# Seeding PSUM bank by bank in a graph-network kernel, with a wait for each bank

## The reference

```python
mask = (adj > 0.0).astype(x.dtype)
xj_proj = x @ W1a
diff = x[:, :, None, :] - x[:, None, :, :]
h = jax.nn.relu(xj_proj[:, :, None, :] + diff @ W1b + b1)
hm = jnp.einsum('bjkh,bjk->bjh', h, mask)
deg = jnp.sum(mask, axis=-1)
return hm @ W2 + deg[..., None] * b2
```

## Time and profile before

| what | value |
|---|---|
| time, median of 3 runs | 905.02 us (904.84 to 905.02) |
| the profiled execution | 904.65 us, of which the span from first to last instruction is 902.6 us |
| busy share | TensorE 96%, VectorE 96%, ScalarE 86%, GpSimd 77% |
| seeds (L530) | 512, 811 ns each |
| granted TensorE clock | 0.983 of full speed |

### The profile page before, as it was taken

The page is one execution under the profiler, slowest core; times in us unless marked ns, Lnnn a source line. Parts: engine busy times, 40 slices in busy tenths (PEclk is TensorE's granted clock), DMA queues, the critical chain, the costliest instruction groups (busy, mean ns, idle before and its releaser), DMA issues.

```text
span 902.6 us, 27715 instructions
## 1 busy us (share of the span) xinstructions
PE 862.0 (96%) x8626; PEld 771.7 (86%) x8627; DVE 866.4 (96%) x3032; ACT 775.9 (86%) x1728; POOL 698.8 (77%) x1548
## 2 busy tenths in 40 slices
PE   3879999999999999999999999999999999999996
PEld 1448999989998989999999999998999899989995
DVE  6989999999999999999999999999999999999993
ACT  4858989898989898989889898988898889898983
POOL 0857787888888888888887878787878788888874
PEclk9789999999999999999999999999999999999997
DMA  9700000000000000000000000000000000000000
GB/s 341 279 1 5 20 11 20 16 20 17 19 17 20 11 20 17 20 17 20 15 14 16 20 17 19 17 18 18 12 20 16 20 16 20 16 20 11 7 8 16
DMA packets 26549, 27.58 MB, mean 31 GB/s; under 512 B 3360, under 2 KB 24352, under 8 KB 25376
## 3 DMA queue, kind: packets, MB, share of 16 engines
q1 hardware_dynamic: 25488, 25.37, 8.3%
q10 hardware_dynamic: 912, 0.39, 0.2%
HBM read 21.56 MB, written 4.19 MB: 29 GB/s over the span
## 4 chain that ended last, share of the span: by engine, by line
PE 69%; DVE 19%; issue 5%; ACT 3%; POOL 2%; DMA 1%; SPq 0%; ACTq 0%; POOLq 0%; DVEq 0%
PE ring L378 36%; DVE acc L763 12%; PE ring L406 6%; PE post L465 4%; PE post L464 4%; PE prep L435 4%; PE post L470 4%; PE prep L445 3%; PE prep L442 2%; DVE onehot_space L749 2%; PE prep L441 2%; ACT ring L530 1%; POOL rstd L915 1%; DMA x_all<-x_nbf_dram 1%; DVE onehot_row L804 1%
## 5 line engine op out<-in xcount | busy, mean ns | idle before, releaser
L763 DVE SCALAR_TENSOR_TENSOR acc<-ring,acc 128x384 f32<-128x384 f32 x896 | 489.0, 546 | 1.1 <-PE ring L378 0.2
L530 ACT COPY ring<-P 128x768 f32<-128x768 f32 x512 | 403.3, 811 | 16.3 <-DVE acc L763 6.9
L378 PE MATMUL ring<-PQ,onehot_space 128*128 128x192 f16 x4096 | 404.0, 247 | 7.2 <-ACT ring L530 3.3
L378 PEld LDWEIGHTS ring<-PQ,onehot_space 128*128 128x128 f16 x4096 | 338.2, 100 | 31.7 <-ACT ring L530 19.2
L864 POOL TENSOR_TENSOR relu_row<-relu_row 128x192 f32<-128x192 f32 x256 | 151.8, 593 | 101.1 <-ACT relu_row L562 91.1
L749 DVE TENSOR_SCALAR onehot_space<-mask_all 128x512 f16<-128x512 f16 x512 | 155.2, 305 | 0.0
L583 ACT ACTIVATE h<-x_all,shift,rstd 128x64 f32<-128x64 f32 x128 | 56.3, 440 | 83.6 <-POOL shift L883 83.6
L851 POOL TENSOR_SCALAR start<-P,spare 128x192 f32<-128x192 f32 x128 | 121.1, 946 | 5.9 <-ACT P L576 5.1
L464 PE MATMUL post<-consts,acc 128*128 128x128 f32 x512 | 98.5, 274 | 1.5 <-POOL relu_row L864 1.5
L465 PE MATMUL post<-ownerT,relu_row 128*128 128x128 f32 x512 | 99.0, 275 | 0.0
L406 PE MATMUL ring<-PQ,owner 128*128 128x384 f16 (+1 forms) x512 | 94.1, 306 | 0.0
(11 more groups left out here) (129 smaller groups left out, 1616.0 us busy)
## 6 DMA issues: line engine op xcount, KB each, us to landing
onehot_space<-adj_kbj_dram SPq DMA_DIRECT2D x8, 1024.0 KB, 17.1
adj_again<-adj_kbj_dram SPq DMA_DIRECT2D x128, 64.0 KB, 1.9
x_all<-x_nbf_dram SPq DMA_DIRECT2D x8, 512.0 KB, 17.8
out_dram<-x_all SPq DMA_DIRECT2D x32, 128.0 KB, 1.7
consts<-consts_dram SPq DMA_DIRECT2D x1, 192.0 KB, 2.6
scratch<-w1a_dram ACTq DMA_DIRECT2D x2, 48.0 KB, 4.3
scratch<-w1b_dram ACTq DMA_DIRECT2D x2, 48.0 KB, 6.7
scratch<-b_dram ACTq DMA_DIRECT2D x1, 96.0 KB, 10.0
```

Of the source, the lines that this page charges most:

```text
L378: last = nc.tensor.matmul(to, hot(s), parts[:, part, H:2 * H], start=False, stop=(part == 1), skip_group_check=True)
L530: return nc.scalar.copy(slots[to], src.unsqueeze(1).unsqueeze(1).broadcast_to([N, BANKS, PER_BANK, H]))
L763: return nc.vector.scalar_tensor_tensor(sums, slots[to][:, bank_], 0.0, start[:, :, :] if first else sums, ALU.max, ALU.subtract if first ...
```

## The change

The seed becomes two copies, one for each bank, each with its own wait ahead of it and its own `seeded`. In chunks 0, 1 and 3 the copy into bank 0 waits for `half_summed` and the copy into bank 1 for `summed`. TensorE waits for `seeded` before each bank's four matmuls. In the looped variant (for graphs with more rows than fit, a branch of its own) the seed becomes two copies as well.

```diff
@@ TensorE, gather of a regular chunk
-                            pe.wait_ge(seeded, b * REGULAR + i + 1)
                             for bank_ in range(BANKS):
+                                pe.wait_ge(seeded, (b * REGULAR + i) * BANKS + bank_ + 1)
                                 dst = [(s, slot(place(u, i), s)) for s in range(PER_BANK * bank_, PER_BANK * (bank_ + 1))]
                                 gather(dst, parts, hot).then_inc(gathered, 1)
@@ ScalarE
-            def seed(to, src):
-
-                return nc.scalar.copy(slots[to], src.unsqueeze(1).unsqueeze(1).broadcast_to([N, BANKS, PER_BANK, H]))
+            def seed(to, src, bank_):
+
+                return nc.scalar.copy(slots[to][:, bank_], src.unsqueeze(1).broadcast_to([N, PER_BANK, H]))
...
-                        if i in (0, 1) and exists(b - 1):
-                            act.wait_ge(summed, b * REGULAR - 1 + i)
                         if i == 2 and exists(b - 1):
                             act.wait_ge(relu_row_ready, b)
-                        if i == 3:
-                            act.wait_ge(summed, b * REGULAR + 1)
-                        seed(place(u, i), P[:, u % 2, :]).then_inc(seeded, 1)
+                        for bank_, consumed in enumerate((half_summed, summed)):
+                            if i in (0, 1) and exists(b - 1):
+                                act.wait_ge(consumed, b * REGULAR - 1 + i)
+                            if i == 3:
+                                act.wait_ge(consumed, b * REGULAR + 1)
+                            seed(place(u, i), P[:, u % 2, :], bank_).then_inc(seeded, 1)
```

More of the change, by code:

```diff
@@ L598, in step @@
                             wait_apart(act, loop_summed, first + k + 1)
-                            seed(place(u, CHUNKS), P[:, u % 2, :]).then_inc(loop_seeded, 1)
+                            seed(place(u, CHUNKS), P[:, u % 2, :], 0)
+                            seed(place(u, CHUNKS), P[:, u % 2, :], 1).then_inc(loop_seeded, 1)
                         wait_apart(act, loop_summed, first + n + 1)
```

## The result

| | before | changed |
|---|---|---|
| median of 16 runs | 905.00 us | 907.31 us |
| range | 904.13 to 906.47 | 904.54 to 908.31 |
| ratio | | 1.0023, 95% interval 1.0015 to 1.0031 |

The changed kernel is 2.3 us slower. That is the forecast direction and inside the forecast range, but less than half of the 5 us that the sum gave. Its first profile was taken in the fastest of its runs, 904.54 us; a second one, in the last experiment, took 907.52 us. The page of the first: part 1, the first lines of part 4 (the chain that ended last), and ScalarE's seeds in part 5.

What follows compares the result with a forecast made beforehand. The prediction took a ScalarE-GpSimd loop of 6.48 us per graph as the bound; minus 0.14 for the wait, plus 2 x 0.09 for splits gave 6.52, plus 5 us over some 125 graphs: 910 us, range 895 to 917.

Steps and rivals of the forecast that it cites:

- the sum: Per graph 6.48 - 0.14 + 2 x 0.09 = 6.52 us, plus 0.04 on some 125 of 128 graphs: plus 5 us.
- The bound: A loop relu_row, GpSimd, h2, h1, two seeds, relu_row takes 6.48 us per graph, 6.34 without the wait for VectorE.
- Term 1: ScalarE's wait for VectorE before the seed of chunk 1 goes: minus 0.14 us per graph.
- Term 3: Each split seed costs ScalarE 0.09 us more; two lie in the loop: plus 0.18 per graph.
- The low end of my bound: A half seed holds ScalarE 0.37 like PQ's copy out of PSUM, so a split costs only 0.005 us.
- the high end: Split cost from the seed's hold less 0.83 to 0.88 ns per element: a fixed part of 0.06 to 0.10 us.
- Terms 2, 4 and 5: TensorE's seed wait vanishes, worth nothing; chunk 2 and 3 seeds 0.18 later are covered; met waits inside a gather cost nothing.
- The fixed 3.67: The time from relu_row through GpSimd's part to h2, taken as unchanged at 3.67 us per graph.

Runs made afterwards that it cites:

- the last experiment: The changed kernel itself run once more, unaltered, for a second profile: 907.77 us against 905.27 for the kernel before, ratio 1.0034.
- the quarters: The changed kernel with the seed of chunk 0 written by four copies of 128x192 instead of two of 128x384: 947.30 us, ratio 1.0455.
- the kernel with h1 moved: ScalarE runs h1 ahead of h2: 868.04 us on the changed kernel, 908.44 on the one before, 873.62 with only chunk 1's seed split.
- the exchange: VectorE's one-hot write of chunk 2 swapped with PQ's second part: 902.12 us on the changed kernel, 928.42 on the one before, 894.59 with only chunk 1's seed split.

## Why the prediction was right or wrong

*The bound, right.* The loops were read as they are. The splits of chunk 0 and of chunks 2 and 3 alone change the time by 0.01% and 0.1%, that of chunk 1 alone gains 1%, and h1's place is worth 39 us only where the seed of chunk 1 is split.

*Term 1, the wait of 0.14, right.* It vanished in each kernel with chunk 1 split: sums_T and the seed stand 0.37 apart in all of them.

*Term 3, the price of a split, right, with some luck.* 0.09 was taken between bounds of 0.005 and 0.10, and the halves measured 0.413 each. By the Trainium skill (ScalarE: Activation LUTs, What ACT_TABLE_LOAD costs) it is 0.413 and 0.093; the trace agrees on these copies out of SBUF, and on the quarters, which hold ScalarE 0.25 each (an estimate by the same figures of the Trainium skill is 0.253). Copies out of PSUM stay at 0.37 for 384 elements, below what the Trainium skill gives. The low end of my bound was such a copy, and was the wrong neighbour. The working of the high end was off as well: the holds of 0.14, 0.37 and 0.48 give 0.86 to 0.90 ns per element, not 0.83 to 0.88, and with them the seed's fixed part is 0.04 to 0.08. The 0.09 is above what these rows support.

*Terms 2, 4 and 5, right.* TensorE moved its wait to h2 (0.23), the idle before h2 fell to 0.42, and met waits inside a gather cost nothing. One size in them was wrong without harm: TensorE's turn without the wait for the seed isn't 6.32, since the kernel with h1 moved turns in 6.20.

*The sum, the failed step: "plus 0.04, on some 125 of the 128 graphs (the first few have no neighbours to wait for)".* The 0.04 measured 6.52 - 6.48 = 0.04 in the ordinary profile. But the first graphs were put at nothing, and they gain. Layer 1 begins three graphs behind layer 0, so in them ScalarE has no h2 to wait for, and ScalarE waits for VectorE before both seeds of the loop. ScalarE's seeds of the third graph before, and then in the second profile of the changed kernel:

```profile
75.94 0.80 ACT L530 COPY ring<-P 128x768 f32<-128x768 f32 x1 [0.88 <-DVE acc L763]
...
78.10 0.80 ACT L530 COPY ring<-P 128x768 f32<-128x768 f32 x1 [0.89 <-DVE acc L763]
78.84 0.65 ACT L562 ACTIVATE relu_row<-ring 128x576 f32<-128x576 f32 x1
```

```profile
74.80 1.09 ACT L530 COPY ring<-P 128x384 f32<-128x384 f32 x2
...
77.11 0.48 ACT L530 COPY ring<-P 128x384 f32<-128x384 f32 x1 [0.18 <-DVE acc L765]
77.53 0.65 ACT L563 ACTIVATE relu_row<-ring 128x576 f32<-128x576 f32 x1
```

Before, the two seeds waited 0.88 and 0.89 us for VectorE; after, 0.18 in one half. The third relu_row starts at 77.53 instead of 78.84, 1.3 us earlier: 0.2 of it stands ahead of the first relu_row, 0.1 comes between the first and the second, and 1.0 between the second and the third.

Not all of this is what the earlier seed gives. With chunk 1 alone split, each of these two distances is 0.33 shorter than before (5.71 for 6.04, 6.82 for 7.15). The rest of the 1.0 is mostly a meeting of VectorE and GpSimd in the kernel before, which the splits happened to move. VectorE's onehot_row and GpSimd's PQ in the third graph before, then onehot_row in the second profile of the changed kernel:

```profile
75.77 0.90 DVE L804 TENSOR_SCALAR onehot_row<-code_row 128x128 f16<-128x128 f16 x3
...
75.72 0.55 POOL L890 TENSOR_TENSOR PQ<-P,PQ 128x192 f16<-128x192 f32 x1
```

```profile
75.30 0.38 DVE L806 TENSOR_SCALAR onehot_row<-code_row 128x128 f16<-128x128 f16 x3
```

Those 0.52 us are lost in the kernel before, and in the one with chunk 1 alone split, where the three instructions take 0.90 too. The kernel with only chunks 2 and 3 split, whose seed of chunk 1 waits as before, has 6.16 there too, as the changed kernel has 6.15. No rule for such meetings was forecast, and this part is chance.

From the third relu_row to the last it is 808.65 us before and 813.07 after, plus 4.4, and the two spans end 2.9 us apart (905.5 against 902.6). So the sum is minus 1.3 for the first graphs, plus 4.4 for the 125 others (0.035 each), and minus 0.2 at the end. The forecast had plus 5 for all. The medians are only 2.3 apart because the profile before lies 0.35 below the median of its runs and this one 0.2 above the other's.

*"The fixed 3.67", named as the place where the loop could be wrong.* Its median is 3.64 and 3.67 in the two profiles of the changed kernel, and 3.66 before, so the forecast survived it; in the kernel with quarters it was 3.84.

## What to carry to other kernels

When a wait is to be taken away, add up the loop that remains without it, start to start, before paying for the removal: here the wait of TensorE was 0.18 us per graph, the loop through VectorE could give 0.14, and two more instructions in the next loop took 0.18. Split only the instruction that waits (chunk 1 alone: 9 us faster), and then look in the new loop for work that doesn't belong there (h1: 39 us together with the split, nothing without it). Then look again at the seeds: once h1 had moved, the whole seed of chunk 0 waited as well. Walk the first graphs apart from the steady ones, since other loops are closed there.

## What the runs showed of the hardware

VectorE and GpSimd hold each other up in both directions, instruction by instruction. VectorE's from_first (128x128, fp16, tensor_scalar) takes 0.22 us when it starts ahead of GpSimd's first sum of relu_row. When it starts behind it, it ends 0.05 after the sum's end, wherever it started: it takes 0.43 when it starts 0.21 behind (the kernel before), and 0.60 when it starts 0.04 behind (the same with the exchange). GpSimd's rstd on one element takes 0.73 when VectorE's owner (two SBUF inputs) comes through in 0.34 beside it, and 0.57 when owner takes 0.37, as in the last graphs, where no VectorE instruction stands beside it. Its shift takes 0.33 when it starts together with a one-hot write, and 0.19 when it starts 0.19 behind it or alone.

The Trainium skill says so (SBUF — State Buffer, SBUF: two separate sides): the pair of ports that they share is locked for a whole instruction by whichever starts first, a GpSimd instruction or one of VectorE in a 2-port mode or with two SBUF inputs, and the other blocks. From_first behind the sum agrees. Owner and rstd agree less: owner loses only 0.03 to an rstd of 0.57. No trace here shows which mode an instruction of VectorE ran in.

What I hadn't expected is the size of it in a full schedule: moving one 0.28 us write cost 22 us in one kernel and gained 5 in another.
